# Quantising of the FFN's weights in attention's last pass, and the experts and the FFN in one block

## The chip, the cores and the metric

The kernel runs on one core of a Trainium2 chip. The metric is the device time of one execution in microseconds: the median of 3 runs is 2886.16 us (2885.0 to 2889.22).

## What is computed

A small language-model tower with 8 x 1024 tokens of width 256, in float32. Reduced to its steps:

```python
h = W.T[tokens]                                    # 8192 rows of 256
h = h + attention_one(layernorm(h))                # 16 heads of 16, scores times tril(k=-1), softmax
h = h + moe(layernorm(h))                          # gate, 4 experts (256 -> 256 -> 256), best two of 4, plus layernorm(h)
h = h + attention_two(layernorm(h))                # keys from x_kv, across the batch of 8
h = h + ffn(layernorm(h))                          # inner width 704

def ffn(x):                                        # every operand is put on the FP4 grid first
    gate, y = q(x) @ q(w_gate).T, q(x) @ q(w_up).T
    return q(silu(gate) * y) @ q(w_down).T

def q(x):                                          # per block of 16 along the last axis
    scale = max(max(abs(block)) / 6, 1e-12)
    return nearest_of(0, .5, 1, 1.5, 2, 3, 4, 6)(abs(block / scale)) * sign(block) * scale
```

w_gate and w_up are 704 x 256, w_down is 256 x 704; the three are the same for all tokens and are quantised once per execution.

## The kernel before

The tokens are 64 tiles of 128 rows; h (128 x 64 x 256) stays in SBUF throughout. Four blocks run after each other, each closed by a barrier over all engines: `attention_one`, `prepare`, `experts_and_attention_two` and `ffn`.

`attention_one` (L259). One pass of it treats 4 heads of one sequence; there are 32 passes, two for each of 16 halves. A plan written out by hand (`window`, L154, and `plan`, L235) puts events at positions among the 36 score slots (`S`) of a pass, and each engine runs through the same list and takes its own part. TensorE makes the transposed scores (L746), ScalarE their exp (L596), GpSimd sets the future to zero with affine selects (L513), TensorE multiplies by the values (`PV`, L766). Beside that the row maxima of the *next* pass are found from a second set of scores (`MX`: TensorE L806, VectorE L693), whose operands Qm and Km SyncE loads from `parts` (L446, L447). A pass's end is done in the following pass: GpSimd's `tmp` (L567), then `PT` on VectorE (acc L717 and reciprocal L720), GpSimd's division (L578), ScalarE's copy of the transposed result (L618), the product with Wr (L854), and its addition to h (`WR`, L724). In the list named `last` the second pass has nothing following: no maxima, no loads. Its end stands in the list `final`. Behind the lists SyncE waits for the last scores and loads four matrices of attention two into `stage` (L457), the memory of the stacked queries and keys.

`prepare` (L897) makes the constants of the other two blocks:
- SyncE's queue: b1 and b2, then xkv and waves, `too`, and the experts' weights.
- ScalarE's queue: w_gate, w_up and w_down (L978 to L981); it has no other work.
- VectorE: b1 and b2 split in bfloat16 pieces, the copy of xkv transposed (L1051), then `scales` (L1018) for the three matrices in turn: largest of each block (L1030), scale (L1031), reciprocal (L1032), times BELOW (L1033), product (L1034), exponent (L1037), half a step of the grid (L1038). For w_gate and w_up GpSimd then adds and subtracts this `power` and multiplies by the scale (L1007, L1009, L1011); for w_down VectorE does (L1066, L1068, L1070). Between them stand the spread of the projections (kp L1059, vb L1062), then mkp (L1073), M (L1077), VO (L1080), and last 36 copies of the transposed weights out of PSUM (L1086, L1088).
- TensorE: transposes xkv (L1096), 96 passes of projections with 8 columns (L1103), the mixing products (L1111, L1115, behind `spread`), and the 36 transposes of the quantised weights (L1126, L1128).

`experts_and_attention_two` (L1133) is a software pipeline: iteration i works on tile i and on tiles up to 6 behind and 4 ahead; iterations -4 to 11 are written out, 12 to 59 are a hardware loop of 4, 60 to 70 are written out. All 8 PSUM banks are its own: mm1, mmT, mm2 (two each), in_ps, sum_ps. `ffn` (L1554) has the same form: steps -7 to 7, a loop of 4, and the last ones. Step i takes statistics of tile i+7, normalises and begins to quantise tile i+3, multiplies tile i by gate and up (L1642) and tile i-3 by down (L1680).

```python
            for k in range(3):
                scales(k)
            dve.wait_ge(proj, 1)
            dve.wait_ge(zeroed, 3)
```

## Time and profile before

The profile is of one execution, which took 2895.28 us. Shares are of its span.

| | |
|---|---|
| median of 3 runs | 2886.16 us |
| the profiled execution | 2895.28 us |
| its span, first to last instruction | 2893.5 us |
| TensorE (PE) busy | 2526.1 us, 87% |
| VectorE (DVE) busy | 2120.3 us, 73% |
| GpSimd (POOL) busy | 1639.9 us, 57% |
| ScalarE (ACT) busy | 1510.1 us, 52% |
| mean granted TensorE clock | 0.947 |

PEld is TensorE's weight load, which overlaps its products. PEclk is the clock granted to TensorE as a share of 2.4 GHz; 0.50 is the lower of its two levels, 1.2 GHz. In the views in order of time, like instructions that follow each other are merged: "x12" are twelve, and the duration is from the first one's start to the last one's end. A line is start us, us, engine, line, operation, out<-in, shapes, count. In brackets stands how long the engine was idle before the instruction and what ended that. SPq and ACTq are DMA issues on the queues of SyncE and ScalarE. The tables by stretch give, for each stretch, its length, the busy us (and instructions) of PE, PEld, DVE, ACT and POOL, PEclk, the DMA engines' busy share and GB/s. Times are from the start of the span.

### The profile page before, as it was taken

The page shows a single profiled execution, that of the slowest core. Times are in us where ns is not written, and L with a number is a line of the kernel's source. Part 1 is how long each engine was busy: PE and PEld are TensorE (multiplying, and loading weights), DVE is VectorE, ACT ScalarE, POOL GpSimd, SP SyncE. Part 2 cuts the span into 40 slices and gives each one's busy share as a digit, 9 for nine tenths or more (in the row PEclk, how much of TensorE's full clock was granted, in tenths as well). Part 3 has the DMA queues.
Part 4 walks back from the last instruction along what each step waited for, and adds up shares of the span by engine and source line. Part 5 has one row for each costly group of instructions (what it writes and reads, how often), then busy time and mean ns, then how long its engine had stood idle before and what let it go on. Part 6 is the DMA issues. An engine that isn't in the chain of part 4 may idle for free. (4 is left out here: it accounts for less than half of the span.)

```text
span 2893.5 us, 58186 instructions
## 1 busy us (share of the span) xinstructions
PE 2526.1 (87%) x15254; PEld 1485.1 (51%) x15318; DVE 2120.3 (73%) x5672; ACT 1510.1 (52%) x3246; POOL 1639.9 (57%) x2560
## 2 busy tenths in 40 slices
PE   3888888888888888888868999999999889999999
PEld 1333334433334433333355666666666656666666
DVE  6667767667677667776467999999999866555564
ACT  1555556555556555556504655555555544444444
POOL 6753333443333443343246878777877667677775
PEclk7899999999999999999869999999999989999999
DMA  4533433433433433443140000000000000000000
GB/s 109 111 72 59 68 59 57 66 58 58 67 60 57 66 58 59 66 67 56 26 142 1 1 1 0 0 0 0 0 0 0 1 6 17 15 16 15 15 16 19
DMA packets 81254, 112.93 MB, mean 39 GB/s; under 512 B 25100, under 2 KB 37144, under 8 KB 80536
## 3 DMA queue, kind: packets, MB, share of 16 engines
q1 hardware_dynamic: 76360, 101.44, 20.5%
q0 software_dynamic: 3072, 8.39, 1.0%
q10 hardware_dynamic: 1744, 2.16, 0.2%
q8 instruction: 36, 0.59, 0.1%
q14 instruction: 42, 0.34, 0.0%
HBM read 18.98 MB, written 8.39 MB: 9 GB/s over the span
## 5 line engine op out<-in xcount | busy, mean ns | idle before, releaser
L693 DVE TENSOR_REDUCE cand<-ring 128x4 f32<-128x512 f32 x1152 | 714.0, 681 | 348.4 <-PE ring L806 326.1
L596 ACT ACTIVATE probs<-scoresT 128x512 f32<-128x512 f32 x1152 | 624.5, 605 | 588.0 <-PE scoresT L746 537.5
L746 PE MATMUL scoresT<-stage 98*128 98x512 bf16 (+3 forms) x1536 | 381.7, 340 | 43.0 <-ACT probs L596 28.8
L513 POOL TENSOR_SCALAR_AFFINE_SELECT probs<-probs 128x256 f32<-128x256 f32 x512 | 203.8, 413 | 319.4 <-ACT probs L596 312.4
L766 PE MATMUL pv<-probs,Vg 128*32 128x512 f32 (+3 forms) x3072 | 330.9, 553 | 17.9 <-POOL probs L513 15.9
L806 PE MATMUL ring<-Km,Qm 64*128 64x512 bf16 (+2 forms) x1792 | 228.6, 321 | 77.7 <-DVE cand L693 40.8
L1238 PE MATMUL mm<-w_W,hT 128*128 128x256 f32 x1024 | 243.6, 381 | 8.4 <-ACT z L1326 3.5
L1258 PE MATMUL mm<-w_W,x2T 128*128 128x512 f32 x512 | 242.2, 595 | 0.3 <-DVE x L1477 0.2
L746 PEld LDWEIGHTS scoresT<-stage 98*128 98x128 bf16 x1536 | 121.9, 99 | 220.7 <-ACT probs L596 130.4
L1319 ACT ACTIVATE hT<-mmT,w_be,w_g 128x128 f32<-128x128 f32 x512 | 185.5, 469 | 76.8 <-PE mmT L1249 76.8
L806 PEld LDWEIGHTS ring<-Km,Qm 64*128 64x128 bf16 x1792 | 76.3, 95 | 269.8 <-issue 130.8
L1238 PEld LDWEIGHTS mm<-w_W,hT 128*128 128x128 f32 x1024 | 195.9, 191 | 31.2
L1680 PE MATMUL down_ps<-q_down,turned 128*128 128x256 f32 (+1 forms) x768 | 201.5, 396 | 2.3 <-ACT turned L1710 2.3
L1734 POOL TENSOR_TENSOR val<-val,power 128x960 f32<-128x960 f32 (+2 forms) x68 | 129.1, 1898 | 112.3 <-ACT power L1721 112.3
L766 PEld LDWEIGHTS pv<-probs,Vg 128*32 128x32 f32 x3072 | 86.1, 116 | 184.1 <-issue 148.5
L1642 PE MATMUL gate<-q_w_gate,turned 128*128 128x352 f32 x512 | 173.9, 462 | 0.7 <-ACT turned L1705 0.5
L1642 PE MATMUL up<-q_w_up,turned 128*128 128x352 f32 x512 | 172.4, 459 | 0.0
L1680 PEld LDWEIGHTS down_ps<-q_down,turned 128*128 128x128 f32 (+1 forms) x768 | 134.9, 189 | 68.2 <-issue 43.4
L1693 ACT ACTIVATE act_g<-gate 128x352 f32<-128x352 f32 x128 | 59.3, 463 | 209.0 <-PE gate L1642 203.1
L1386 POOL TENSOR_TENSOR u<-z,w_g 128x512 f32<-128x512 f32 x128 | 160.2, 1273 | 1.7 <-ACT z L1326 1.7
L1326 ACT ACTIVATE z<-mm,nmw,rw 128x256 f32<-128x256 f32 x256 | 123.6, 565 | 58.7 <-POOL nmw L1403 58.5
L1258 PEld LDWEIGHTS mm<-w_W,x2T 128*128 128x128 f32 x512 | 98.2, 192 | 87.5 <-issue 83.3
(255 smaller groups left out, 5269.4 us busy)
## 6 DMA issues: line engine op xcount, KB each, us to landing
stage<-parts SPq DMA_DIRECT2D x256, 96.0 KB
Qm<-parts SPq DMA_DIRECT2D x128, 128.0 KB
Km<-parts SPq DMA_DIRECT2D x128, 128.0 KB
stage<-parts SPq DMA_DIRECT2D x256, 64.0 KB
stage<-parts SPq DMA_DIRECT2D x256, 32.0 KB
out<-result SPq DMA_DIRECT2D x64, 128.0 KB, 1.7
stage<-ct SPq DMA_DIRECT2D x128, 4.0 KB
w_W<-in_W SPq DMA_DIRECT2D x4, 512.0 KB
```

Of the source, the lines that this page charges most:

```text
L513: nc.gpsimd.affine_select(out=d, in_=d, compare_op=ALU.is_gt, fill=0.0, base=0, pattern=[[0, 2], [1, P]], channel_multiplier=-1).then_inc( ...
L596: nc.scalar.activation(probs[:, buffer(slot), :], scoresT[slot % SCORE_BANKS][:], ACT.Exp, scale=SOFT).then_inc(exp_ok, 1)
L693: ins = nc.vector.tensor_reduce(c, src[:].rearrange("p (t a b) -> p t a b", t=c.shape[1], b=P), AX.X, ALU.max)
L746: ins = nc.tensor.matmul(scoresT[slot % SCORE_BANKS][:, at:at + hi - lo], Ks[0:ROWS, gi, hh, P * kt:P * kt + P], Qs[0:ROWS, gi, hh, lo:hi] ...
L766: ins = nc.tensor.matmul(pv[32 * hh:32 * hh + 32, lo:512], Vg[:, par, kt, hh, :], probs[:, buffer(slot), column:column + 512 - lo], start= ...
L806: ins = nc.tensor.matmul(out[x][:, P * at:P * (at + n)], Qm[half[x], hh // 2, P * i:P * i + P], Km[half[x], hh // 2, P * j:P * (j + n)], s ...
L1238: ins = nc.tensor.matmul(o, hT[:, 2 * e + c, :], w["W2"][:, c, e, :], start=False, stop=(e % 2 == 1 and c == 1))
L1258: ins = nc.tensor.matmul(mm1[p][:], x2T[same][:, c, :], w["W1"][:, c, 2 * p:2 * p + 2, :].rearrange("p e n -> p (e n)"), start=False, stop ...
L1319: nc.scalar.activation(hT[:, j, :], mmT[p][:, P * k:P * k + P], ACT.Relu, bias=w["be1"][:, j:j + 1], scale=w["g1"][:, j:j + 1]).then_inc(h ...
L1386: nc.gpsimd.tensor_tensor(u[same][:, 2 * p:2 * p + 2, :], z[same][:, 2 * p:2 * p + 2, :], w["g2"][:].rearrange("p (e n) -> p e n", e=E4)[: ...
L1642: ins = nc.tensor.matmul(out[:, 0:HALF], turned[par][:, 5 + c, :], wt[:, c, HALF * a:HALF * a + HALF], start=(c == 0), stop=(c == 1))
L1680: ins = nc.tensor.matmul(down[:, 0:D], turned[1 - u][0:rows, at, :], w["down"][0:rows, k, :], start=(n == 0), stop=(n == CHUNKS - 1))
```

## The change

- A new tensor `hold` (128 x 8192) lives through the whole kernel. In attention one it holds `parts`, xn, xT, f32part, Qm and Km. The second pass of the list `last` gets three new kinds of event (`weights=True`): `LOAD_W` at position 0 (SyncE loads the three matrices into `hold` once the last pass's first scores are made; VectorE fills the padding), `FP4` three times at position 9 (VectorE, one matrix each), and `FP4_GRID` at position 15 (GpSimd, w_gate's three passes). VectorE now does these passes for w_up as well as for w_down.
- `prepare` loses the loads, the quantising and GpSimd's passes. TensorE's transposes are divided over the block: banks 0 and 1 first, 2 and 3 behind the projections, the other 8 at the end. The copies of even banks (of 4 transposes) go to ScalarE, of odd banks (of 2) to VectorE; ScalarE also takes one half of the spread and VO. xkv and waves are loaded first.
- `ffn` no longer has a block. It returns its steps, which the experts' block runs: step i - 68 behind iteration i for i from 61 to 69 on each engine, and the others behind the last iteration. It has the experts' PSUM banks, `stage` and the free part of `hold`; hN, hT, z and u of the experts lie in `hold`. New waits (`banks_read`, `small_read`, `tiles_done`) guard what is shared.

The events and the quantising in attention:

```diff
+FP4 = {"w_gate": (0, 6 * D, 0), "w_up": (6 * D, 6 * D, 1), "w_down": (12 * D, 2 * FFN, 0)}
+POWER_AT, SCALE_AT, HOLD = (4608, 6144), 7680, 8192
...
+    if weights:
+        at(0, ("LOAD_W",))
+        at(pos_of["WR"] + 7, *(("FP4", k) for k in range(len(FP4))))
+        at(15, ("FP4_GRID",))
...
+                        elif e[1] == "LOAD_W":
+                            for s in (q_in[1], k_in[1]):
+                                sp.wait_ge(s, 16 * 12 * HALVES)
+                            sp.wait_ge(st_ok, UNITS * (2 * HALVES - 1) + 1)
...
+                        elif kind == "FP4_GRID":
+                            v, up, n = quantised(hold, "w_gate"), raised[0], FP4["w_gate"][1]
+                            pool.wait_ge(fp4_scaled, 1)
+                            nc.gpsimd.tensor_tensor(v, v, up[:, 0:n], ALU.add).then_inc(fp4_grid, 1)
+                            pool.wait_ge(fp4_grid, 1)
+                            nc.gpsimd.tensor_tensor(v, v, up[:, 0:n], ALU.subtract).then_inc(fp4_grid, 1)
+                            pool.wait_ge(fp4_grid, 2)
+                            nc.gpsimd.tensor_tensor(blocks(v), blocks(v), each(scales[0], P, n // BLOCK), ALU.mult).then_inc(fp4_grid, 1)
...
+                            dve.wait_ge(fp4_in[k], 16 if name == "w_down" else 32)
+                            link(nc.vector.tensor_reduce(s, blocks(v), AX.X, ALU.max, apply_absolute_value=True), 1)
+                            link(nc.vector.tensor_scalar(s, s, SIXTH, TINY, ALU.mult, ALU.max), 2)
+                            link(nc.vector.reciprocal(r, s), 3)
+                            link(nc.vector.tensor_scalar(r, r, BELOW, None, ALU.mult), 4)
+                            link(nc.vector.tensor_tensor(blocks(v), blocks(v), each(r, P, n // BLOCK), ALU.mult), 5)
+                            if name == "w_down":
+                                dve.wait_ge(fp4_grid, 2)
+                            link(nc.vector.tensor_scalar(up.bitcast(U32), v.bitcast(U32), EXPONENT, None, ALU.bitwise_and), 6)
+                            ins = nc.vector.tensor_scalar(up, up, 1.0, HALF_STEP, ALU.max, ALU.mult)
+                            if name == "w_gate":
+                                ins.then_inc(fp4_scaled, 1)
+                            else:
+                                link(ins, 7)
+                                link(nc.vector.tensor_tensor(v, v, up, ALU.add), 8)
+                                link(nc.vector.tensor_tensor(v, v, up, ALU.subtract), 9)
+                                nc.vector.tensor_tensor(blocks(v), blocks(v), each(s, P, n // BLOCK), ALU.mult)
```

`prepare`, ScalarE's new work, VectorE's and TensorE's order:

```diff
+                keep_even(0)
+                act.wait_ge(proj, 1)
+                act.wait_ge(zeroed, 2)
+                spread_half(copy, 0).then_inc(spread, 1)
+                keep_even(2)
+                act.wait_ge(mixed, 2)
+                copy(w["VO"][:], ps[3][:, 0:D])
+                for b in range(4, len(banks), 2):
+                    keep_even(b)
...
+                keep_odd(1)
+                dve.wait_ge(turned, 1)
+                nc.vector.tensor_copy(xkvT[:], ps[0][:, 0:2 * KEYS].rearrange("p (c j) -> p c j", c=2)).then_inc(turned_sb, 1)
                 dve.wait_ge(rows_in, 32)
...
-                for k in range(3):
-                    scales(k)
                 dve.wait_ge(proj, 1)
                 dve.wait_ge(zeroed, 3)
...
+                spread_half(nc.vector.tensor_copy, 1).then_inc(spread, 1)
+                keep_odd(3)
...
+                turns(0, 2)
                 pe.wait_ge(kv_in, 16 * len(KV))
...
+                turns(2, 4)
+                pe.wait_ge(spread, 2)
...
+                turns(4, len(banks))
```

The merged block:

```diff
+        AMONG = {TILES - 3: -7, TILES - 2: -6, TILES - 1: -5, TILES: -4, TILES + 1: -3, TILES + 2: -2, TILES + 3: -1, TILES + 4: 0, TILES + 5: 1}
+        banks = {"gate": (mmT[1], mm2[0]), "up": (mm1[1], mm2[1]), "four": in_ps, "rest": mmT[0], "down": sum_ps, "small": mm1[0]}
...
             for i in range(LAST_LOOP, TILES + BEHIND):
                 run(i, i % 2)
+                if i in AMONG:
+                    run_ffn(AMONG[i], AMONG[i] % 4, AMONG[i] // 4 + 1)
+            following["rest"](eng, run_ffn, 1 + AMONG[TILES + 5])
...
-            prepare(nc, dram, w, wf, staged, staged_in)
-            experts_and_attention_two(nc, dram, h, w)
-        ffn(nc, dram, h, wf)
+            prepare(nc, dram, w, wf, staged, staged_in, hold)
+            experts_and_attention_two(nc, dram, h, w, wf, stage, hold)
```

## Rows read from the trace of the kernel before

**Rows 1.** Table by stretch: twelve us of the experts' loop, and the FFN
```profile
2236.00:2248.00 12.00, 11.17 (x55) 8.05 (x55) 11.79 (x48) 7.13 (x20) 9.58 (x18) 1.00 0.00 0
...
2400.00:2893.00 493.00, 488.39 (x2049) 339.41 (x2047) 277.83 (x556) 228.12 (x399) 345.48 (x198) 1.00 0.05 16
```

**Rows 2.** In order of time, attention's last pass to its end
```profile
1429.41 0.69 DVE L724 TENSOR_TENSOR h<-ring,h 128x512 f32<-128x512 f32 x1 [0.36 <-PE ring L854]
...
1443.86 0.41 POOL L513 TENSOR_SCALAR_AFFINE_SELECT probs<-probs 128x256 f32<-128x256 f32 x1 [12.96 <-ACT probs L596]
...
1451.60 0.44 DVE L717 TENSOR_TENSOR acc<-ring,tmp 128x272 f32<-128x272 f32 x1 [21.50 <-PE ring L846]
...
1454.58 3.69 PE L854 MATMUL ring<-w_r,OT 128*128 128x256 f32 x16
...
1458.31 0.69 DVE L724 TENSOR_TENSOR h<-ring,h 128x512 f32<-128x512 f32 x1 [0.17 <-PE ring L854]
```

**Rows 3.** In order of time, `prepare`, VectorE on w_gate alone
```profile
1468.55 1.75 DVE L1030 TENSOR_REDUCE s_w_gate<-v_w_gate 128x96 f32<-128x1536 f32 x1
...
1470.33 0.21 DVE L1031 TENSOR_SCALAR s_w_gate<-s_w_gate 128x96 f32<-128x96 f32 x1
...
1471.62 1.76 DVE L1034 TENSOR_TENSOR v_w_gate<-v_w_gate,i_w_gate 128x1536 f32<-128x1536 f32 x1
...
1474.40 0.96 DVE L1038 TENSOR_SCALAR power<-power 128x1536 f32<-128x1536 f32 x1
```

**Rows 4.** In order of time, `prepare`, GpSimd on w_gate, VectorE on w_up
```profile
1475.45 3.43 POOL L1007 TENSOR_TENSOR v_w_gate<-v_w_gate,power 128x1536 f32<-128x1536 f32 x1 [9.16 <-DVE power L1038]
...
1477.06 1.89 DVE L1031 TENSOR_SCALAR s_w_up<-s_w_up 128x96 f32<-128x96 f32 x1
...
1479.77 2.68 DVE L1033 TENSOR_SCALAR i_w_up<-i_w_up 128x96 f32<-128x96 f32 x1
...
1482.46 2.81 POOL L1011 TENSOR_TENSOR v_w_gate<-v_w_gate,s_w_gate 128x1536 f32<-128x1536 f32 x1
...
1482.48 4.40 DVE L1034 TENSOR_TENSOR v_w_up<-v_w_up,i_w_up 128x1536 f32<-128x1536 f32 x1
```

**Rows 5.** In order of time, `prepare`, VectorE's last pass over w_down
```profile
1507.18 1.63 DVE L1070 TENSOR_TENSOR v_w_down<-v_w_down,s_w_down 128x1408 f32<-128x1408 f32 x1
```

**Rows 6.** In order of time, `prepare`'s start and TensorE's chain, to the experts' start
```profile
1460.18 1.19 SPq L958 DMA_DIRECT2D rows<-in_b  x2
...
1468.04 0.38 PE L1096 MATMUL prep<-ident,xkv 8*128 8x8 f32 x2 [9.77 <-DMA waves<-in_waves]
...
1468.68 1.03 PE L1103 MATMUL prep<-xkvT,stage 128*128 128x8 f32 x4 [0.27 <-DVE xkvT L1051]
...
1503.89 7.04 PE L1111 MATMUL prep<-kp,stage 128*128 128x32 f32 x32 [14.55 <-DVE vb L1062]
...
1510.73 6.02 PE L1115 MATMUL prep<-too,vb 128*128 128x256 f32 x16
...
1521.72 2.45 DVE L1086 COPY q_down<-turn 128x128 f32<-128x128 f32 x12
...
1524.47 1.40 POOL L1369 TENSOR_TENSOR h<-h,w_br 128x256 f32<-128x256 f32 x2 [25.73 <-SPq L1223]
```

**Rows 7.** Table by stretch, during the projections (columns as in rows 1)
```profile
1470.00:1480.00 10.00, 10.00 (x48) 10.00 (x49) 9.69 (x11) 0.00 (x0) 4.47 (x2) 0.50 1.04 329
```

**Rows 8.** DMA issues of the page: KB each, us to landing
```profile
out<-result SPq DMA_DIRECT2D x64, 128.0 KB, 1.7
```

**Rows 9.** In order of time, from experts to FFN
```profile
2324.66 0.42 DVE L1548 TENSOR_TENSOR h<-sum_ps,h 128x256 f32<-128x256 f32 x1 [2.36 <-PE sum_ps L1289]
...
2335.48 2.71 PE L1642 MATMUL gate<-q_w_gate,turned 128*128 128x352 f32 x4 [0.47 <-ACT turned L1705]
```

**Rows 10.** Table by stretch, the experts' tail and the FFN's start
```profile
2290.00:2325.00 35.00, 22.60 (x75) 15.56 (x74) 23.52 (x71) 10.97 (x33) 14.57 (x29) 0.65 0.00 1
...
2325.00:2335.00 10.00, 0.68 (x2) 0.29 (x2) 7.63 (x29) 1.85 (x4) 3.89 (x7) 0.50 0.00 1
```

More of the change, by code:

```diff
@@ L972, in _, with keep @@
                 sp.wait_ge(loaded, 16 * (len(LOADS) + 1))
+            def keep(copy, b):
+                n, c, parts = banks[b]
+                src = turn[b % 4]
+                for at, (k, lo, rows_) in enumerate(parts):
+                    if n == "w_down":
+                        ins = copy(wf["down"][0:rows_, k, P * c:P * c + P], src[0:rows_, P * at:P * at + P])
+                    else:
+                        ins = copy(wf[n][:, c, P * k:P * k + rows_], src[:, P * at:P * at + rows_])
+                return ins
@@ new lines, in sb, with sem, wait, two @@
+    def sb(name, shape, dt=F32):
+        return ctx.enter_context(nc.sbuf_tensor(name, shape, dt))
+    def sem(name):
+        return ctx.enter_context(nc.semaphore(name))
+    def wait(eng, s, value):
+        if isinstance(value, int) and value <= 0:
+            return
+        eng.wait_ge(s, value)
+    def two(name, shape, dt=F32):
+        return [sb(f"{name}_{a}", shape, dt) for a in range(2)]
+    st, mv, rs = sb("f_st", [P, UNROLL, 6]), sb("f_mv", [P, UNROLL, 2]), sb("f_rs", [P, UNROLL])
@@ new lines, in ffn, with staged @@
+    act_g = [spare[:, INNER * n:INNER * (n + 1)].rearrange("p (a n) -> p a n", a=2) for n in range(2)]
+    at = [0]
+    def staged(n):
+        at[0] += n
+        return stage[:, at[0] - n:at[0]]
+    comb, val, grid = ([staged(WIDE) for _ in range(2)] for _ in range(3))
+    power, square = [staged(WIDE // 2).bitcast(BF16) for _ in range(2)], staged(WIDE // 2).bitcast(BF16)
+    result = [staged(D) for _ in range(2)]
+    scale, lift = two("scale", [P, NB]), sb("lift", [P, 1])
+    turned = two("turned", [P, 8, P])
@@ new lines, in group, with sync @@
+    def group(g):
+        return not isinstance(g, int) or 0 <= g < TILES // UNROLL
+    def sync(sp):
+        for t in range(2):
+            sp.wait_ge(result_ok, t + 1)
+            sp.dma_start(dram["out"][P * t:P * t + P, :], result[t][:]).then_inc(stored[t], 16)
+        with sp.Fori(1, TILES // 2) as j:
+            for a in range(2):
+                sp.wait_ge(result_ok, 2 * j + a + 1)
+                sp.dma_start(dram["out"][bass.ds(2 * P * j + P * a, P), :], result[a][:]).then_inc(stored[a], 16)
+        for a in range(2):
+            sp.wait_ge(stored[a], 16 * (TILES // 2))
@@ new lines, in gpsimd, with run @@
+    def gpsimd(pool):
+        def run(i, a4, g):
+            u, r = a4 % 2, i + 2
+            due = on(r, 0) or on(r, BEHIND)
+            lo, hi = columns(r)
+            v, e = val[u][:, lo:hi], power[u][:, lo:hi]
+            if due:
+                pool.wait_ge(power_ok, r + 1)
+                nc.gpsimd.tensor_tensor(v, v, e, ALU.add).then_inc(lifted, 1)
+            if a4 == 0 and group(g):
+                wait_apart(pool, (mv_ok, g + 1))
+                nc.gpsimd.tensor_scalar(rs[:], mv[:, :, 1], EPS, None, ALU.add).then_inc(eps_ok, 1)
+                pool.wait_ge(eps_ok, g + 1)
+                nc.gpsimd.tensor_tensor(rs[:], rs[:], w["minus_half"][:], ALU.pow).then_inc(rs_ok, 1)
+            if due:
+                pool.wait_ge(lifted, r + 1)
+                nc.gpsimd.tensor_tensor(v, v, e, ALU.subtract).then_inc(lowered, 1)
+                pool.wait_ge(lowered, r + 1)
+                wait(pool, rest_ok, r - 1)
+                wait(pool, four_ok, r - 1 - BEHIND)
+                nc.gpsimd.tensor_tensor(blocks(grid[u][:, lo:hi]), blocks(v),
+                                        each(scale[u][:, lo // BLOCK:hi // BLOCK], P, (hi - lo) // BLOCK), ALU.mult).then_inc(grid_ok, 1)
+        return run
```

591 lines of the change are left out of this document (262 added, 329 removed).

## The prediction

> **What bounds the kernel now.** The tables by stretch come first. In the experts' loop VectorE is busy for 11.79 of 12 us, in the FFN from 2400 us on TensorE for 488 of 493 us [rows 1]. Neither loop loses an instruction, so nothing is won in them; the chain of waits says only that the FFN ends last on TensorE. What can move are the two seams, where neither engine is full, and these were read line by line in time order.
>
> First seam. Attention's last instruction, the fourth add of h on VectorE, ends at 1459.0 [rows 2]; `prepare` begins at 1460.2 and the experts at 1524.5, 64.3 us later [rows 6]. In these lie VectorE's quantising of three matrices [rows 3 to 5] and TensorE's projections, which wait 14.55 us for VectorE behind L1103 [rows 6]. In attention's last pass VectorE has no maxima left and idles for 21.5 us until 1451.6 [rows 2]. Second seam. The experts' last add ends at 2325.1, the FFN's first gate product starts at 2335.5 [rows 9].
>
> **Part 1: quantising in the last pass of attention.** VectorE can begin behind its last WR add, at 1430.1 [rows 2]. Its own work: w_gate takes 1468.55 to 1475.36, 6.8 us undisturbed [rows 3]. w_up is as wide, 6.8, plus the three passes that VectorE now does itself: over w_down's 1408 columns they take 1.63 each [rows 5], over 1536 columns 1.78, so 5.4; 12.2 in all. w_down is 6.8 x 1408/1536 = 6.2, and 3 x 1.63 + gaps = 4.95; 11.2. Sum 30.2 us, against 21.5 us of idle time.
>
> GpSimd's three passes over w_gate come on top: 1475.45 to 1485.27, 9.8 us, now from 1436.9 on. Beside them VectorE's instructions stretch, in this order: 1.89 and 2.68 us for steps of 96 columns that take 0.21 alone, 4.40 for the product that takes 1.76 [rows 3, 4]. Added: 1.68 + 2.47 + 2.64 = 6.8. The same instructions meet again, so I keep it. Chain: 1430.1 + 30.2 + 6.8 = 1467.1.
>
> Then the masks. GpSimd's wait for w_gate and its three passes stand in its queue ahead of the masks of slots 27 to 35: eight of 0.41 us (one affine select), the first at 1443.9 before [rows 2], now from about 1446.9, and the product `tmp`, about 1.1 us. ScalarE waits for none of them; TensorE's last two bursts do, and they are done well before VectorE is free. No row shows whether an affine select holds VectorE up as a two-input pass does. Bounds: 0, or 8 x 0.41 + 1.1 = 4.4 us. I take 3.0, as VectorE is then in just the kinds of instruction that stretch in [rows 4], less what falls beside reductions. The Trainium skill (SBUF — State Buffer, section "Who interferes with whom") says that a VectorE instruction with two SBUF inputs and a GpSimd instruction that reads SBUF shut each other out whole. By it the masks would cost nearly the 4.4. The trace agrees for the passes [rows 4]; no row shows it for masks.
>
> So VectorE reaches `acc` (L717) at 1470.1 instead of 1451.6: 18.5 us late, and all of attention's tail waits behind it. That tail took 7.4 us [rows 2] with TensorE's granted clock at its upper level. TensorE now stops for some 9 us ahead of it; behind the stop before the projections its clock is 0.50, the lower level [rows 7]. The 16 products of 256 columns in `prepare` took 6.0 us, mostly at that level [rows 6], the 16 of the tail 3.7 [rows 2]. +2.3 us; bounds 0 and 2.7. `prepare` begins 20.8 us later, at 1481.0. The weights' loads (five DMAs, 2.1 MB) go through SyncE's queue from the last pass's first scores on, some 11 us ahead of their use, and `prepare`'s staged loads behind them start as before; if that cover fails, the chain moves by the delay.
>
> **Part 2: `prepare` without it.** TensorE's chain sets the end. xkv and waves are now first in SyncE's queue. Before, TensorE got them 7.9 us after the block's start, behind 1.4 MB of weights [rows 6]. Two issues (about 1 us) and the 1.7 us in which a DMA lands in the FFN [rows 8] give 2.7; I take 3.2, bounds 2.7 and 7.9. Transposing and copying xkv: 1.0 (0.6 of it up to L1103). L1103: 1468.7 to 1489.3, 20.6 us, at 0.50 though TensorE never paused [rows 6, 7]; kept. Six weight transposes at that clock beside the spread, halved between two engines: 2. L1111 and L1115: 1503.9 to 1516.75, 12.9 [rows 6]. Last, 24 transposes; ScalarE copies 16 of the 24. VectorE takes 0.2 per copy (twelve in 2.45 [rows 6]); I take that for ScalarE too, and 4 us with VO's copy, bound 6. Sum 43.7, less 0.4 of overlap: 43.3. The experts start at 1524.3 instead of 1524.5. **The first seam gives nothing**: the 21.0 us that leave `prepare` come back as 20.8 in attention's tail.
>
> **Part 3: experts and FFN in one block.** The FFN's steps -7 to 1 stand behind the experts' iterations 61 to 69 in each queue. From 2290 to 2325 VectorE is busy for 23.5 of 35 us, and from 2325 to 2335, the FFN's start, for 7.6 of 10 [rows 10]. If the FFN's work fitted wholly into the gaps, 10 us would go; if none did, nothing but the change of block (0.4, from 2325.1 to the FFN's first statistics). Walked down the queues: the statistics in steps -7 to -4 push VectorE by 1.1 us, the aggregates by 0.5; steps -3, -2, -1 take 2.0 us each. While VectorE does them, TensorE, ScalarE and GpSimd run ahead through the next iteration's transposes, copy and VO, which were VectorE's waits before. Iterations 65, 66 and 67, 7.0, 4.6 and 3.3 us apart before, then end at 2312.4, 2319.1 and 2323.9, and the first gate product comes at 2327.2: 8.3 us sooner. Then iteration 69's VO product waits for a ScalarE copy that is queued behind the second Silu, a square and a power, and holds the FFN's step 1 by 1.6 us. Net **6.7 us**; bounds 3 and 10.
>
> The padding fills on VectorE (it idles there) and the new semaphores cost nothing. Sum: 0 + 6.7 us less. The profiled execution took 2895.28 us, 1.8 more than its span; the median of the runs is 2886.16, 9.1 less than the profiled one. The profiled one should come to 2888.6, the median to 2879.5.
>
> **Rivals.**
> 1. More is won: masks do not stretch VectorE (3.0), the tail keeps the upper clock (2.3), and the projections run partly at it; at the upper level they would take half of 20.6 us, and half of that gain is 5. 2879.5 - 10 = 2869. Against it: 0.50 through 20.6 us of unbroken work [rows 7]. The Trainium skill (TensorE: Matmul & The Clock Gate, part 1) says that sustained activity releases the clock; by it the projections would run at the upper level for most of their length and the time be about 2869 as well. The rows speak against it for products of 8 columns.
> 2. The merge gives little: VectorE is the common queue, so each FFN step lengthens the experts' tail by its whole length. Only the change of block is saved, 0.4 of 6.7: 2885.8. For it: VectorE is already the busiest engine there.
> 3. Slower, by the experts' loop. hN, hT, z and u move to other addresses, and the block's programme grows. With VectorE at 11.79 of 12 us [rows 1] nothing absorbs a longer instruction. From (6.7 + 5.8)/56 = 0.22 us per tile on the kernel is slower; 0.3 gives 2896. Against it: instructions, shapes and banks of the loop are the same.
> 4. The change does what it says and hides all quantising: 30.2 us would have to fit into 21.5. It would give about 2860.
>
> **How the numbers follow.** A measurement of this kernel tells about 0.2%, 5.8 us, from no change: faster is below 2880.4, slower above 2891.9. Forecast 0.52, rival 1 0.17, rival 2 0.20, rival 3 0.10, rival 4 0.01. The forecast's bounds are masks -3.0/+1.4, clock -2.3/+0.4, landing -0.5/+4.7, merge -3.3/+3.7, not all met together: 2873 to 2886, six tenths of it below 2880.4. Faster: 0.31 + 0.17 + 0.01 = 0.49; slower 0.10 + 0.01 = 0.11; same 0.40. Range 2867 to 2890: rivals 1 and 2 with a margin; rival 3, rival 4 and the far end of 1 are left out.
>
> **What the changed profile would show.** VectorE at `acc` of the last pass near 1470 with hardly any idle time before it; masks of slots 27 and later between VectorE's passes; L1103's products 20.6 us long at 0.50; `prepare` 43 us; the experts' start within 3 us of 1524.5; the first gate product 2 us behind the experts' last add instead of 10. I am wrong if `acc` comes before 1465 or after 1474, if another engine than TensorE sets `prepare`'s end, or if a tile of the experts takes another time.

## The result, and the profile of the changed kernel

The changed kernel takes 2896.93 us (median of 12 runs, 2887.43 to 2901.37), the kernel before 2885.82 beside it (12 runs, 2881.71 to 2890.38). The ratio is 1.0035, with a 95% interval of 1.0024 to 1.0045: **slower by 0.35%**, about 10 us. The forecast was 2879.5, with a range up to 2890. The profiled execution of the changed kernel took 2896.81 us, its span is 2895.1 us, its mean granted clock 0.946.

The two profiled executions can't be laid side by side from 0 on. Attention reaches the last WR add ahead of its tail (the addition of an output projection to h, L724 before, L801 after; the tail has four more) at 1429.41 us before [rows 2] and at 1422.20 after, and in the profiles of the experiments below that point lies anywhere between 1421 and 1438 with the same instructions ahead of it. So time is counted from the start of that add, in three stages: from it to the experts' first VectorE instruction (the first seam), from there to the FFN's first product with w_down, the down product (the experts' loop and the second seam), and from there to the end.

| us | before | after |
|---|---|---|
| last WR add to experts' start | 95.1 | 89.9 |
| experts' start to first down product | 833.6 | 847.7 |
| first down product to end of span | 535.3 | 535.4 |

**The first seam**, changed kernel, in order of time. Lines are start us, us, engine, line, operation, out<-in, shapes, count, and in brackets the engine's idle time ahead and what ended it.

```profile
1422.20 0.69 DVE L801 TENSOR_TENSOR h<-ring,h 128x512 f32<-128x512 f32 x1 [0.36 <-PE ring L931]
...
1431.30 1.92 DVE L724 TENSOR_SCALAR hold<-hold 128x96 f32<-128x96 f32 x1
...
1434.04 2.71 DVE L726 TENSOR_SCALAR hold<-hold 128x96 f32<-128x96 f32 x1
1436.78 4.39 DVE L727 TENSOR_TENSOR hold<-hold 128x1536 f32<-128x1536 f32 x1
...
1439.51 10.42 POOL L549 TENSOR_SCALAR_AFFINE_SELECT probs<-probs 128x256 f32<-128x256 f32 x8
...
1441.21 1.04 DVE L730 TENSOR_SCALAR hold<-hold 128x1536 uint32<-128x1536 uint32 x1
...
1443.36 1.84 DVE L736 TENSOR_TENSOR hold<-hold 128x1536 f32<-128x1536 f32 x1
...
1460.49 0.43 DVE L794 TENSOR_TENSOR acc<-ring,tmp 128x272 f32<-128x272 f32 x1
...
1462.06 1.94 PE L927 MATMUL ring<-ident,O 128*128 128x128 f32 x8 [7.57 <-POOL O L622]
1463.92 4.63 PE L931 MATMUL ring<-w_r,OT 128*128 128x256 f32 x16
...
1472.37 0.29 PE L1158 MATMUL prep<-ident,xkv 8*128 8x8 f32 x2 [1.02 <-DMA waves<-in_waves]
...
1494.95 7.03 PE L1174 MATMUL prep<-kp,stage 128*128 128x32 f32 x32
...
1501.80 6.16 PE L1178 MATMUL prep<-too,vb 128*128 128x256 f32 x16
...
1512.06 0.30 DVE L1498 MEMSET wt<- 128x128 f32 x2 [0.47 <-PEq L1024]
```

VectorE goes from the last WR add straight through the three matrices to `acc`, 37.6 us from 1422.9 to 1460.49. Beside GpSimd's three passes it is stretched by the sizes of [rows 4] (1.92, 2.71, 4.39). Beside the masks it is hardly: 1.04 instead of 0.96, 1.84 instead of about 1.76. The one that is stretched there is GpSimd, whose eight masks take 10.42 us instead of 0.41 each. TensorE does wait for them, 10.05 us ahead of L843, but it is through at 1454.5, 6 us before VectorE reaches `acc`: the delay costs nothing.

**The second seam**, where the FFN's first steps now stand among the experts' last, answers to [rows 9]:

```profile
2335.45 1.78 PE L1719 MATMUL mmT<-q_w_gate,turned 128*128 128x352 f32 x4
...
2343.54 0.43 DVE L1627 TENSOR_TENSOR h<-sum_ps,h 128x256 f32<-128x256 f32 x1 [0.65 <-PE sum_ps L1368]
...
2359.72 3.15 PE L1759 MATMUL sum_ps<-q_down,turned 128*128 128x256 f32 x12
```

The first gate product now starts 8.1 us ahead of the start of the experts' last add; before it started 10.8 us behind it [rows 9]. From the last tile's transposes of the experts' hidden layer (2297.98, before 2290.00) to the first down product it is 61.7 us instead of 68.2.

**The experts' loop** holds the loss. First the table by stretch (length, busy us and instructions of PE, PEld, DVE, ACT and POOL, PEclk, DMA share, GB/s), one stretch ahead of the loop's first jump back and one with two jumps back in it:

```profile
1640.00:1700.00 60.00, 55.99 (x267) 40.53 (x271) 59.01 (x230) 35.69 (x100) 48.02 (x91) 1.00 0.01 2
1700.00:1760.00 60.00, 53.29 (x250) 37.71 (x253) 53.40 (x209) 34.70 (x96) 46.25 (x88) 0.99 0.00 1
```

Then the waits of VectorE between 1560 and 2280 us (tile and line that waited, releaser, us in total, times, longest), and one of them in order of time:

```profile
DVE gy L1515 <- issue: 26.7, 11, 2.6
DVE hold L1601 <- POOL rsA L1442: 10.7, 58, 0.5
DVE lg L1529 <- issue: 3.6, 11, 0.6
```
```profile
2004.14 0.41 DVE L1627 TENSOR_TENSOR h<-sum_ps,h 128x256 f32 x1
2007.02 0.16 DVE L1515 SCALAR_TENSOR_TENSOR gy<-rank,gx 128x4 f32<-128x4 f32 x1 [2.46 <-issue]
2007.15 1.93 DVE L1519 TENSOR_REDUCE both<-hold 128x256 f32<-128x1024 f32 x1
2009.00 0.14 DVE L1522 TENSOR_REDUCE gsum<-gy 128x1 f32<-128x4 f32 x1
2009.43 0.29 DVE L1529 TENSOR_TENSOR lg<-in_ps,w_neg 128x128 f32<-128x128 f32 x1 [0.28 <-issue]
```

"issue" says that the engine waited for nothing that the profile shows. L1515 is VectorE's first line in the loop body; of 64 executions of it, 11 have the stall, one per jump back, which is the branch at a round's end to its first instruction (the loop has 12 rounds of 4 tiles). The kernel before has no such wait: its L1436, the same instruction, starts behind its predecessor without idle time. And in the page's list of DMA queues the one that carries instructions, q14, moves more than twice as much (packets, MB, share of 16 engines), first after, then before:

```profile
q14 instruction: 97, 0.79, 0.1%
```
```profile
q14 instruction: 42, 0.34, 0.0%
```

Between 1640 and 2240 us alone it is 59 packets after and 6 before.

### The profile page after: what moved, and what is told of

It is laid out like the page before. It is cut to its first block and busy times, and to the rows that moved or that the text cites. A ratio compares the mean times of both kernels' runs of the same rounds, so it can differ in the third digit from the quotient of the medians.

```text
span 2895.1 us, 58170 instructions
## 1 busy us (share of the span) xinstructions
PE 2542.4 (88%) x15254; PEld 1491.5 (52%) x15318; DVE 2102.9 (73%) x5641; ACT 1514.9 (52%) x3280; POOL 1633.5 (56%) x2557
## 5 line engine op out<-in xcount | busy, mean ns | idle before, releaser
L843 PE MATMUL pv<-probs,Vg 128*32 128x512 f32 (+3 forms) x3072 | 337.5, 563 | 28.2 <-POOL probs L549 25.2
L883 PE MATMUL ring<-hold 64*128 64x512 bf16 (+2 forms) x1792 | 227.4, 321 | 75.4 <-DVE cand L770 44.2
L1317 PE MATMUL mm<-w_W,hold 128*128 128x256 f32 x1024 | 247.2, 385 | 7.2 <-ACT hold L1405 2.8
L1398 ACT ACTIVATE hold<-mmT,w_be,w_g 128x128 f32<-128x128 f32 x512 | 185.6, 469 | 77.7 <-PE mmT L1328 77.7
L1317 PEld LDWEIGHTS mm<-w_W,hold 128*128 128x128 f32 x1024 | 198.6, 194 | 32.5
L1759 PE MATMUL sum_ps<-q_down,turned 128*128 128x256 f32 (+1 forms) x768 | 201.5, 396 | 2.3 <-ACT turned L1788 2.3
L1811 POOL TENSOR_TENSOR stage<-stage 128x960 f32<-128x960 f32 (+2 forms) x68 | 129.0, 1898 | 109.5 <-ACT stage L1799 109.5
L843 PEld LDWEIGHTS pv<-probs,Vg 128*32 128x32 f32 x3072 | 86.8, 118 | 197.1 <-issue 146.7
L1719 PE MATMUL mm<-q_w_up,turned 128*128 128x352 f32 x512 | 173.6, 462 | 0.0
L1759 PEld LDWEIGHTS sum_ps<-q_down,turned 128*128 128x128 f32 (+1 forms) x768 | 134.9, 189 | 68.2 <-issue 43.4
L1465 POOL TENSOR_TENSOR hold<-hold,w_g 128x512 f32<-128x512 f32 x128 | 160.7, 1277 | 0.8 <-ACT hold L1405 0.8
L1405 ACT ACTIVATE hold<-mm,nmw,rw 128x256 f32<-128x256 f32 x256 | 123.6, 566 | 55.6 <-POOL nmw L1482 55.3
L1836 DVE TENSOR_TENSOR stage<-hold,mm 128x352 f32<-128x352 f32 x128 | 66.3, 518 | 93.3 <-PE mm L1719 93.2
L1819 POOL TENSOR_TENSOR stage<-stage 128x960 f32<-128x960 f32 (+2 forms) x68 | 129.3, 1902 | 4.2
```

The source lines that it names most:

```text
L843: ins = nc.tensor.matmul(pv[32 * hh:32 * hh + 32, lo:512], Vg[:, par, kt, hh, :], probs[:, buffer(slot), column:column + 512 - lo], start= ...
L883: ins = nc.tensor.matmul(out[x][:, P * at:P * (at + n)], Qm[half[x], hh // 2, P * i:P * i + P], Km[half[x], hh // 2, P * j:P * (j + n)], s ...
L1317: ins = nc.tensor.matmul(o, hT[:, 2 * e + c, :], w["W2"][:, c, e, :], start=False, stop=(e % 2 == 1 and c == 1))
L1398: nc.scalar.activation(hT[:, j, :], mmT[p][:, P * k:P * k + P], ACT.Relu, bias=w["be1"][:, j:j + 1], scale=w["g1"][:, j:j + 1]).then_inc(h ...
L1465: nc.gpsimd.tensor_tensor(u[same][:, 2 * p:2 * p + 2, :], z[same][:, 2 * p:2 * p + 2, :], w["g2"][:].rearrange("p (e n) -> p e n", e=E4)[: ...
L1719: ins = nc.tensor.matmul(out[:, 0:HALF], turned[par][:, 5 + c, :], wt[:, c, HALF * a:HALF * a + HALF], start=(c == 0), stop=(c == 1))
```

## The theories and what tells them apart

- **P, position.** VectorE's instructions are fetched again at each jump back, because of where the loop lies in its instruction stream. In the built programs the loop's body is 306 instructions for VectorE in both kernels (waits and register instructions counted). It begins at instruction 1375 before and at 1342 after: the moved quantising added 31 instructions to attention's end, and the split of `prepare` took 64 away.
- **M, merge.** The FFN's code in the same block does it.
- **A, addresses.** The experts' arrays in `hold` make VectorE wait; that was rival 3 of the prediction.

## The experiments

In the table the stages are those of above, each from one profile; "start" is VectorE's instruction at which the experts' loop begins, and its remainder by 256. The ratio to the kernel before has its 95% interval where the run was timed.

| run | start | stall at the loop's head, us x times | first seam | experts to down | ratio |
|---|---|---|---|---|---|
| before | 1375, 95 | none | 95.1 | 833.6 | |
| after | 1342, 62 | 2.4 x 11 | 89.9 | 847.7 | 1.0035 (1.0024 to 1.0045) |
| e1, 33 writes | 1375, 95 | none | 90.2 | 827.6 | 0.9944 (0.9928 to 0.9959) |
| e2, without merge | 1342, 62 | 2.4 x 11 | 90.1 | 856.4 | 1.0053 (1.0036 to 1.0070) |
| e3, merge alone | 1375, 95 | none | 93.8 | 827.2 | 0.9972 (0.9960 to 0.9985) |
| e4, loop from 16 | 1554, 18 | none | 90.1 | 825.3 | 0.9954 (0.9940 to 0.9969) |
| e5, before, loop from 16 | 1587, 51 | 2.4 x 10 | 93.7 | 849.5 | 1.0054 (1.0039 to 1.0069) |
| e6, 2 tiles a round | 1342, 62 | none | 90.1 | 828.4 | 0.9972 (0.9960 to 0.9984) |
| e7, 8 writes | 1350, 70 | none | 90.1 | 825.3 | |
| e8, 20 writes | 1362, 82 | none | 90.0 | 827.3 | |
| e9, 4 writes | 1346, 66 | 2.5 + 2.1 x 11 | 90.2 | 872.1 | |
| e10, loop from 16, 6 writes | 1560, 24 | 3.1 x 10 | 90.1 | 852.6 | |
| e14, loop from 16, 3 writes | 1557, 21 | 3.5 x 10 | 90.0 | 852.6 | |
| e15, 7 writes | 1349, 69 | 4.8 x 11 | 90.2 | 876.3 | |
| e11, w_gate on VectorE, 6 writes | 1350, 70 | none | 87.7 | 827.7 | |
| e12, wide products, 8 writes | 1350, 70 | none | 93.2 | 825.5 | 0.9967 (0.9954 to 0.9980) |
| e13, loop from 16, w_gate on VectorE | 1556, 20 | none | 87.7 | 827.4 | 0.9936 (0.9921 to 0.9951) |

The last stage is 535.3 or 535.4 us in every run.

**e1: shift the loop and nothing else.** The writes stand where VectorE waits for TensorE's first products in `prepare`.

```diff
+        pad = sb("pad", [P, 33])
...
+                for k in range(33):
+                    nc.vector.memset(pad[0:1, k:k + 1], 0.0)
                 dve.wait_ge(proj, 1)
```

> The changed kernel with 33 one-element writes on VectorE in the preparation, where VectorE waits for TensorE's first products; nothing else. In the built program the experts' loop then begins at VectorE's instruction 1375, where it begins in the kernel before, and no longer at 1342; its body is 306 instructions in both. Theory P (position): VectorE's 2.4 us stall at the head of 11 of the loop's 12 rounds comes from where the loop lies in VectorE's instruction stream: it is fetched again at each jump back. Then the stalls are gone, the instruction queue that moved 97 packets moves about 42, the experts' stage falls from 786 to about 766 us, and the ratio to the kernel before is 0.9965 (0.995 to 0.998; 2896.9 - 20.5 = 2876 us). Rival M (merge): the FFN's in-line code in the same block does it: stalls stay, ratio 1.0035 (1.002 to 1.005). Rival A (addresses): the experts' arrays in the common tensor make VectorE wait: as M, 1.0035.

33 writes that compute nothing make the kernel faster: 0.9944. VectorE's waits between 1560 and 2280 us are now

```profile
DVE hold L1604 <- POOL rsA L1445: 12.7, 60, 1.2
DVE x L1559 <- POOL rs L1445: 0.5, 1, 0.5
```

and q14 has 42 packets again. The experts' stage is 20.1 us shorter than in the changed kernel. Theory P holds, M and A fall: both said that the stalls stay. As only VectorE's stream was shifted, the 55 packets were VectorE's. The ratio is below the range that was expected (0.995 to 0.998), which is taken up at the end of the next section. Stalls of 30.3 us cost 20.1 (20.0 to 22.4 against the other undisturbed runs with the merge and this loop body, which take 825.3 to 827.7 us). In order of time the changed kernel's tiles start 14.4 to 14.8 us apart where there is a stall, the next one 11.3 to 12.3, and then two some 12.0; with the 33 writes all are 11.9 to 12.2 apart, as in the kernel before. So about a third of the stalls comes back. Between 1700 and 2200 us two VectorE groups are shorter on average than in e1: the changed kernel's L1556 with 636 ns against 773, its L1559 (L1562 in e1) with 525 against 697. That GpSimd got ahead in the stall and is out of their way is argued, not shown.

**e2 and e3: each half of the change alone.** e2 takes the FFN out into its own block again, e3 does only the merge:

```diff
 e2, from the changed kernel
-            experts_and_attention_two(nc, dram, h, w, wf, stage, hold)
+            experts_and_attention_two(nc, dram, h, w, hold)
+        ffn(nc, dram, h, wf)
```
```diff
 e3, from the kernel before
-            experts_and_attention_two(nc, dram, h, w)
-        ffn(nc, dram, h, wf)
+            experts_and_attention_two(nc, dram, h, w, wf, stage, wsb("hold", [P, 7680]))
```

> The changed kernel without the merge: quantising in attention's last pass, the split preparation and the experts' arrays in the common tensor stay; the FFN has its own block, banks and tensors again as in the kernel before. VectorE's experts' loop begins at instruction 1342, as in the changed kernel. Theory P: the 11 stalls stay; first seam -5, loop +20.5: ratio 1.0053 (1.003 to 1.007). Rival M: without the merge no stalls: ratio 0.998 (0.996 to 1.000). Rival A: as P here.

> The kernel before with the merge alone: experts and FFN in one block, banks and arrays shared, as in the changed kernel; attention's last pass and the preparation as before. VectorE's experts' loop begins at instruction 1375, as in the kernel before. Theory P: no stalls, only the merge's gain of 6.4 us: ratio 0.9978 (0.996 to 0.999). Rivals M and A: stalls, +20.5 - 6.4: ratio 1.0049 (1.003 to 1.007).

1.0053 and 0.9972. The stalls come with the half whose loop has the same instructions as before, with its arrays in `hold`, and not with the merge, which has these arrays in `hold` too. The experts' stage of e2 is 22.8 us longer than before's. In e2, between 1560 and 2280 us:

```profile
DVE gy L1487 <- issue: 26.6, 11, 2.6
DVE hold L1573 <- POOL rsA L1414: 12.3, 59, 1.2
DVE lg L1501 <- issue: 3.9, 11, 0.5
```

e3 has no such line, and its experts' stage is 6.4 us shorter than before: that is the merge. Its first seam, and e5's, is of the same code as before's and takes 93.8 and 93.7 us, so the 95.1 of the profile that the prediction used was 1.4 us long (VectorE idled 21.50 us ahead of L717 there, 19.89 in e3). The 1.4 us are one burst of TensorE's L766 at 1437.48, 3.32 us long at a mean granted clock of 0.58, where e3 and e5 have 1.92 us.

**e4 and e5: one constant, in both kernels.**

```diff
-    FIRST_LOOP, LAST_LOOP, UNROLL = 12, TILES - BEFORE, 4
+    FIRST_LOOP, LAST_LOOP, UNROLL = 16, TILES - BEFORE, 4
```

> The changed kernel with one constant changed: the experts' loop on all engines takes over at iteration 16 instead of 12 (11 rounds in place of 12, four more tiles written out before it). VectorE's loop then begins at instruction 1554 of its stream. Theory P with lines of 256 instructions, of which two are held: a body of 306 fits two lines at most places (1554 is 18 past 1536 by this count; where the lines really begin is not known, only that 1375 is a good place and 1342 a bad one, so that good places are at least those 33 to 239 past the bad one, modulo 256; 1554 is 212 past it): no stalls, ratio 0.9965 (0.995 to 0.998). Rivals M and A: 10 stalls, 1.003.

> The kernel before with the same constant changed: the experts' loop takes over at iteration 16 instead of 12. VectorE's loop then begins at instruction 1587, that is 245 past the changed kernel's 1342, or 11 short of it modulo 256, by the built program. Theory P with lines of 256: a body of 306 needs three lines at 50 of 256 places. 1342 (62 modulo 256) is bad, 1375 (95) and 1554 (18) are good, so the bad stretch begins at 19 to 46 and ends at 67 to 94 (it holds 62); 1587 is 51 modulo 256 and lies in it wherever it begins. So the constant that cured the changed kernel spoils the kernel before: 10 stalls of 2.4 us on VectorE in the experts' loop, about 92 packets in the instruction queue, +18.6 us less some 2 us that fewer rounds gave in the changed kernel: ratio 1.0057 (1.003 to 1.008). Rival M (something of the change itself, which the padding upset by luck): no stalls, 0.999.

The constant cures the changed kernel (0.9954) and spoils the kernel before (1.0054). In e5, between 1560 and 2280 us:

```profile
DVE gy L1436 <- issue: 24.5, 10, 2.5
DVE hN L1522 <- POOL rsA L1363: 9.6, 48, 0.5
```

None of the change is in e5. The 2 us that its expectation took for fewer rounds are not there: e7, with all 12 rounds, has e4's 825.3 us, and undisturbed runs of either kind spread from 825.3 to 827.7.

**e6: a short body.**

```diff
-    FIRST_LOOP, LAST_LOOP, UNROLL = 12, TILES - BEFORE, 4
+    FIRST_LOOP, LAST_LOOP, UNROLL = 12, TILES - BEFORE, 2
```

> The changed kernel with the experts' loop made of 2 tiles a round instead of 4 (24 rounds; VectorE's loop body 160 instructions instead of 306, and it begins at 1342 as in the changed kernel). Theory P: 160 instructions lie in two lines of 256 wherever they begin, so no stall: ratio to the kernel before 0.9965 (0.994 to 0.999), a little dearer than with padding for twice the loop heads. Rival C (a jump back costs VectorE the fetch whatever the body's length): 23 stalls, about +40 us: 1.010.

0.9972, and no stall in 23 jumps back at a start that is bad for the long body. So a jump by itself costs nothing that can be seen; body and place together do.

**e7 to e10, e14, e15: where the edges are.** All are e1 with other counts of writes; e10 and e14 have the constant of e4 too.

> The changed kernel with 8 one-element writes on VectorE in the preparation: the experts' loop begins at 1350 (70 modulo 256). One look, for the place of the edge. By theory P the bad stretch ends somewhere in 67 to 94: likely still bad (11 stalls of 2.4 us, 97 packets).

> As the one with 8, with 20 writes: the loop begins at 1362 (82 modulo 256). Bad with 11 stalls, or good with none; theory P gives even odds, and excludes anything between (a stall of another length or in some rounds alone, apart from how much of the third line must be waited for: near the edge the loop's last instructions lie in the third line, so the stall at the loop's head should not shrink towards it).

> The changed kernel with 4 one-element writes on VectorE in the preparation: the experts' loop begins at 1346 (66 modulo 256). One look. 62 and 51 were bad, 70, 82, 95 and 18 good. If a loop of 306 instructions is bad where it touches three lines of 256, 49 places in a row are bad; with 18 and 70 good and 51 and 62 bad they begin at 19 to 21 and end at 67 to 69. So 66 is bad: 11 stalls of 2.4 us, 97 packets, experts' stage to the first down product 847.7 us and not 827. A bad stretch much shorter than a line's remainder (lines of another length, or another cause) would make it good.

> The changed kernel with the loop from iteration 16 and 6 one-element writes: the loop begins at 1560 (24 modulo 256), 6 instructions past the place 1554 (18) that was good. By the same count 24 is bad: 10 stalls of 2.4 us, 96 packets, about +19 us against the run without the 6 writes. By any other account in which 18 is good, six writes of 0.06 us do nothing: no stalls.

> The changed kernel with the loop from iteration 16 and 3 one-element writes: the loop begins at 1557, 21 modulo 256. By the line account only the jump itself (instruction 306 of the body) lies in the third line, and that is enough: 10 stalls of some 2.5 us at the loop's head and about 96 packets. If fetching ahead were so quick that the jump alone costs nothing, or the lines were a little longer: no stalls, 44 to 47 packets.

> The changed kernel with 7 one-element writes: the loop begins at 1349, 69 modulo 256. By the line account its first instruction alone lies in the first line: the jump back must fetch that line for one instruction and the next line right behind: 11 stalls, of 4 to 5 us together at the loop's head as with 4 writes (2.5 + 2.1 us), 97 packets, experts' stage about 870 us. With 8 writes (70) there was none.

Each was run once. The guess for e7 was wrong (70 is good), and that narrowed the edge: with 18 good, the bad starts had to end at 67 to 69. From there on every start did as forecast: 66, 24, 21 and 69 bad, 20 (e13) good. Of all the runs, 21, 24, 51, 62, 66 and 69 are bad, and their neighbours 20 and 70 are good. That is the count of stretches of 256 instructions: a body of 306 fits into two where it begins 0 to 206 past the start of one, and the other 49 starts make it touch a third. At the upper edge a single write decides, 825.3 us in e7 against 876.3 in e15. The sizes were forecast less well. e9 lost 45 us against a good start, not 20, since it has a second stall; e10 and e14 lost 27 us against e4, where 19 had been expected for e10, with stalls of 3.1 and 3.5 us instead of 2.4 and 2.5.

The traces show the border itself. A stretch begins at remainder 70. From 62 that is the body's ninth instruction, and the changed kernel's small second stall comes right behind it, at L1529. From 66 it is the fifth, the reduction L1522 of e9:

```profile
2025.56 0.41 DVE L1630 TENSOR_TENSOR h<-sum_ps,h 128x256 f32 x1
2028.44 0.16 DVE L1518 SCALAR_TENSOR_TENSOR gy<-rank,gx 128x4 f32<-128x4 f32 x1 [2.46 <-issue]
2030.58 1.90 DVE L1522 TENSOR_REDUCE both<-hold 128x256 f32<-128x1024 f32 x1 [1.97 <-issue]
```

and from 69 it is the second, so that both fetches stand ahead of the body's first shown line, as one stall (e15):

```profile
2077.18 0.16 DVE L1518 SCALAR_TENSOR_TENSOR gy<-rank,gx 128x4 f32<-128x4 f32 x1 [5.13 <-issue]
```

With a start of 24 in e10 the border lies at the body's 47th instruction and at the 303rd, and there the two small stalls are:

```profile
2016.22 0.42 DVE L1628 TENSOR_TENSOR h<-sum_ps,h 128x256 f32 x1 [0.27 <-issue]
...
2020.09 0.26 DVE L1518 SCALAR_TENSOR_TENSOR gy<-rank,gx 128x4 f32<-128x4 f32 x1 [3.12 <-issue]
...
2026.12 0.42 DVE L1579 TENSOR_TENSOR h<-both,h 128x256 f32 x1 [0.35 <-issue]
```

The Trainium skill (Runtime: NRT & Kernel Launch, section "Instruction fetch mechanics") says that most engines hold 512 instructions as two lines of 256, and that a taken branch to an address outside them waits for the fetch. The runs agree: stretches of 256, and a stall once three are touched. Not settled is what exactly moves: q14 has 55 packets and 0.45 MB more in 11 jumps, 5 packets of 8 KB for each, where three stretches of 256 instructions would be 6 if an instruction has 64 bytes, as the Trainium skill (Vector Engine (DVE) Microarchitecture Reference, section 1.2) says.

**e11: w_gate's last passes on VectorE.** Would the first seam be better without GpSimd's help?

```diff
-        at(15, ("FP4_GRID",))
...
-                            if name == "w_gate":
-                                ins.then_inc(fp4_scaled, 1)
-                            else:
-                                link(ins, 7)
+                            link(ins, 7)
```

> The changed kernel with w_gate's three last passes (add, subtract, scale) on VectorE instead of GpSimd, and with 6 one-element writes, so that the loop begins at 1350, a good place. One look, for the last pass of attention: GpSimd's three passes stretched VectorE's L724, L726 and L727 of w_up by 6.8 us (1.91, 2.71 and 4.40 us instead of 0.21, 0.21 and 1.76); on VectorE they cost 3 x 1.84 = 5.5 us. From the last output-projection add to the first acc add 37.0 us instead of 38.3. If GpSimd's masks take the port's place as the disturber: 38 to 41 us. No stalls in the experts' loop.

Yes. From the last WR add to `acc` it is 36.5 us instead of 38.3, and the seam is 87.7 instead of 90.1. The rest of the difference has two signs: the tail takes 9.7 us instead of 8.8 to 9.0, after TensorE was idle for 11.99 us instead of 7.57, and `prepare` 41.4 instead of 42.8. VectorE's w_up product in it:

```profile
1450.47 1.76 DVE L726 TENSOR_TENSOR hold<-hold 128x1536 f32<-128x1536 f32 x1
...
1450.78 7.62 POOL L548 TENSOR_SCALAR_AFFINE_SELECT probs<-probs 128x256 f32<-128x256 f32 x5 [1.44 <-ACT probs L639]
```

The product, 4.39 us beside GpSimd's pass, is 1.76 beside a mask, and it is the masks that take 7.62 us for five. Even GpSimd's two-input `tmp` is the one that is stretched here, to 2.63 us from 1.13, beside VectorE's L732, which started 0.2 us before it and takes 1.84. GpSimd's help cost 6.8 us to save 5.3.

**e12: can the projections have the upper clock?**

```diff
+                ident_16 = w["ident"][:].bitcast(BF16)
+                def wide(n):
+                    for _ in range(n):
+                        nc.tensor.matmul(ps[3][:, 0:2 * P], ident_16[:, 0:P], ident_16, start=True, stop=True)
...
                 turns(0, 2)
+                wide(8)
...
+                        if (a, k) < (PAIRS - 1, 2):
+                            wide(2)
```

> The changed kernel with 8 one-element writes (good place) and, on TensorE in the preparation, 8 + 46 extra bf16 products of 256 columns, whose result is written over: 8 while it waits for the small loads, two behind each pair of the 48 eight-column products. It adds work. The preparation's products ran at a granted clock of 0.50 (20.6 + 7.0 + 6.2 us). If wide products bring the clock to 1.0: extra 46 x 0.11 = 5 us, the 48 products 10 to 15 us, the rest 7 us instead of 13: the preparation is 36 us instead of 41.6, and the ratio 0.9935. If the clock stays at 0.50: extra 46 x 0.21 = 10 us, preparation 51 us, ratio 0.9985.

Only at first. TensorE's busy us, granted clock, DMA share and GB/s in three stretches:

```profile
1480.00:1490.00 10.00, 7.77 (x44) 0.91 0.10 12
1490.00:1500.00 10.00, 10.00 (x68) 0.61 1.03 355
1500.00:1510.00 10.00, 10.00 (x57) 0.50 0.11 20
```

Without the extra products the projections ran at 0.50 from their first one on. With them four take 0.51 us up to about 1492, then 0.86: the clock fell to its lower level while TensorE was busy without a pause, with 256-column products between the narrow ones. The seam is 93.2 instead of 90.1 us, 3.1 more, between the two forecasts (6 less, 9 more); nothing is won.

**e13: what is left when all of this is used.** It is e4 and e11 together, without writes.

> The changed kernel with the experts' loop from iteration 16 and w_gate's three last passes on VectorE; no padding. The loop begins at 1556, that is 20 modulo 256: its last instruction, the jump back, is then the last of the second line. By the line account good, with no instruction to spare: no stalls. Sum from the kernel before: first seam -5.2, w_gate's passes -1.7, merge -6.4, later loop start -2: -15.3 us, ratio 0.9947 (0.993 to 0.9965). If the edge is elsewhere: 10 stalls, 1.001.

2869.31 us (median) beside 2885.49, ratio 0.9936 (the two medians alone give 0.9944): faster than both kernels. It stands on the last good start; one instruction more on VectorE anywhere ahead of the loop puts it at the start of e14, where the stalls are.

## Why the prediction was wrong

**What failed** is the first paragraph's step from "neither loop loses an instruction" to "nothing is won in them", taken as nothing lost either, and with it what stood against rival 3, "instructions, shapes and banks of the loop are the same". They are the same, and a tile still takes another time, because an instruction costs also what it takes to fetch it. Rival 3 had the size and the place (a slowdown by the experts' loop, 2896 us, chance 0.10) but a wrong mechanism, so its hit was luck: e1 and e3 have the new addresses and the block's larger programme and no stall, e5 has neither of them and stalls. The programme ahead of the loop became 33 instructions shorter. Its price was 20.1 us, 0.42 us for each of the loop's 48 tiles, where the rival put 0.3 for each of 56 crossings.

The trace of before shows neither where the stretches of 256 begin nor what a stall costs. But by the account that the runs bear out 49 of 256 starts are bad for a body of 306, so any edit that shifts VectorE's stream had a chance of about one in five to cost 20 us or more (up to 51, e15 against e7), more than everything else in the sum. The last line of the forecast, "if a tile of the experts takes another time", named the right reading.

**Point by point**, against the seams of the runs, which agree to 0.4 us:

- *Quantising chain.* Forecast 40.0 us from 1430.1 to `acc`, measured 37.6. Own work (30.2) and the stretching by GpSimd's passes (6.8) held. The masks were priced at 3.0 between bounds of 0 and 4.4, and cost 37.6 - 30.2 - 6.8 = 0.6. The price of nearly 4.4 that the prediction drew from the Trainium skill (SBUF — State Buffer, section "Who interferes with whom") is not borne out: here it is GpSimd that waits. The section leaves that open, as it says that the order of issue decides who waits.
- *Tail at the lower clock.* Forecast 7.4 + 2.3 = 9.7; measured 8.8 to 9.0 (9.7 and 9.8 in e11 and e13, where TensorE was idle longer), so 1.4 to 1.6 more than before, and the 16 projections of L931 took 4.63 us instead of 3.69 [rows 2].
- *`prepare`.* Forecast 43.3 from the block's start and 44.5 from attention's last add, measured 42.8 from that add. TensorE got xkv and waves about 2.0 us after its start, not 3.2. The projections took 20.6 us at 0.50 as forecast, and L1174 with L1178 13.0 (forecast 12.9). TensorE set the block's end, as forecast.
- *First seam together.* Forecast -0.2, measured 90.1 against the 93.7 of e3 and e5: -3.6. The three small terms all lay on the same side. Against the profile that was used it would be -5.0; 1.4 of that was that profile's own. Counted from the last WR add, the experts start 5.2 us before the forecast's 1524.5, outside the 3 us that it allowed.
- *Merge.* Forecast -6.7, measured -6.4 (e3) and -6.0 (e1). Both steps of it held: the first gate product 8.3 us sooner by the walk down the queues, 8.0 measured from the last tile's transposes (37.5 us instead of 45.5); 1.6 given back, 1.5 measured. One sign failed: the first gate product was to come 2 us behind the experts' last add and came 8.1 ahead of it, because that add itself comes 10.9 us later than before (45.6 instead of 34.7 us behind the last tile's transposes). What that costs is at most the 1.5 us that are given back.
- *FFN.* Nothing, and nothing it was.

Sum of the stages: -3.6 - 6.0 + 20.1 = +10.5 us, ratio 1.0036; measured 1.0035. Without the loop's stalls it would be -9.6, against the forecast of -6.7, and rival 1, which gave -16.7, lay further off. The measured ratio of e1, 0.9944, is -16 us and would fit rival 1's number, but not its mechanism: only the masks came out nearly as it said, the tail lost most of what it wanted to keep, and the projections stayed at 0.50.

What stays open: e1 and e13 were measured 7 and 6 us faster than their stages say (-9.5 us gives 0.9967, -12.2 gives 0.9958), and the upper ends of their intervals (0.9959, 0.9951) just miss that. The stages don't cover attention up to the last WR add, whose length spreads by 17 us between profiles of the same instructions; whether part of the difference sits there wasn't tried. Nor is it known why undisturbed runs of the same body take 825.3 us or some 827.5.

## What to carry to other kernels

When an edit adds or removes instructions ahead of a long hardware loop, count that engine's instructions, waits and register instructions too, up to the loop and in its body: a body that touches three stretches of 256 is fetched again in every round. In a trace look at the head of each round for an idle time that ends with "issue", and at the packets of the instruction queues; the remedy is a shorter body, or a start moved by some instructions. And if one stage's loss has an unlikely cause but a price above the whole sum, it belongs in the range with its chance, even where no row speaks for it.

## What the runs showed of the hardware

- VectorE's loop of 306 instructions stalls at each jump back for 2.4 us from starts in the middle of the bad stretch, for 3.1 and 3.5 us at its lower end (24 and 21), and for 4.6 to 4.8 us at its upper end (66 and 69), where two fetches stand one behind the other. A third stretch that holds the jump alone (21) is enough.
- A two-input pass on GpSimd stretches VectorE's product of 1536 columns from 1.76 to 4.39 us and its one-input steps of 96 columns from 0.21 to 1.92 and 2.71 us. GpSimd's affine selects hardly do (1.84 instead of 1.76 us); they are stretched themselves, from 0.41 to 1.3 us (mean of 8 beside VectorE's passes) and 1.5 us (5 in 7.62). In e11 a two-input pass of GpSimd that started 0.2 us behind VectorE's was stretched too, from 1.13 to 2.63 us.
- A granted clock of 0.50 held for 20.6 us of unbroken 8-column products, and with 256-column products between them and no pause it still fell from its upper to its lower level (0.91, 0.61, 0.50 in three stretches of 10 us).
